# Attention stage: weighted sums in two halves, maxima turned on VectorE, output normalised on GpSimd by feature, jumps announced

## What is computed

```
h = layernorm(x) * (1 + ca) + sa
Q, K, V = lora_linear(h, ...)          # (4, 2048, 16 heads, 16)
scores = Q K^T / sqrt(16) + 0.5**head * (pos_k - pos_q)
attn = softmax(scores, axis=-1)        # over 2048 keys
out = lora_linear(attn V, Wo, bo, Ao, Bo)
x = x + ga * (h + rezero * out)
```

## Time and profile before

| | us |
|---|---|
| median of 3 runs (5603.05 to 5615.82) | 5609.89 |
| the profiled execution, its own time | 5616.02 |
| its span | 5614.2 |
| TensorE (PE) busy, of the span | 5090.5 (91%) |
| VectorE (DVE) busy | 4278.1 (76%) |
| ScalarE (ACT) busy | 3127.8 (56%) |
| GpSimd (POOL) busy | 1232.7 (22%) |

### The profile page before, as it was taken

The page is one execution under the profiler, slowest core; times in us unless marked ns, Lnnn a source line. Parts: engine busy times, 40 slices in busy tenths (PEclk is TensorE's granted clock), DMA queues, the critical chain, the costliest instruction groups (busy, mean ns, idle before and its releaser), DMA issues. The chain is left out here.

```text
span 5614.2 us, 90199 instructions
## 1 busy us (share of the span) xinstructions
PE 5090.5 (91%) x27025; PEld 2743.7 (49%) x27025; DVE 4278.1 (76%) x6749; ACT 3127.8 (56%) x5877; POOL 1232.7 (22%) x959
## 2 busy tenths in 40 slices
PE   5859999999999999999999878987799999956998
PEld 3723333333333333333333367776565555645666
DVE  4768888888888888888888768787798898974000
ACT  1317777777777777777778623232444445433111
POOL 1310000000000000000000033333565666643222
PEclk8959999999999999999999989998889899956999
DMA  4850222202222022220222121112000000034443
GB/s 138 288 122 6 35 57 35 49 13 35 57 35 48 14 35 57 34 47 15 35 57 34 33 55 34 45 34 67 24 18 19 26 18 19 25 130 146 149 147 101
DMA packets 226907, 328.00 MB, mean 58 GB/s; under 512 B 58516, under 2 KB 176527, under 8 KB 216697
## 3 DMA queue, kind: packets, MB, share of 16 engines
q1 hardware_dynamic: 214300, 264.56, 19.8%
q0 software_dynamic: 12224, 58.43, 2.8%
HBM read 195.90 MB, written 134.59 MB: 59 GB/s over the span
## 5 line engine op out<-in xcount | busy, mean ns | idle before, releaser
L667 DVE TENSOR_REDUCE at_mxp<-at_ps_m 128x2 f32<-128x1024 f32 x2098 | 2462.4, 1218 | 379.8 <-PE at_ps_m L726 373.9
L617 ACT ACTIVATE at_prob<-at_ps_s 128x512 f32<-128x512 f32 x4100 | 2114.3, 603 | 482.8 <-PE at_ps_s L716 481.9
L716 PE MATMUL at_ps_s<-at_qs,at_ks 51*128 51x512 f32 x4100 | 1443.1, 477 | 27.7 <-issue 17.0
L716 PEld LDWEIGHTS at_ps_s<-at_qs,at_ks 51*128 51x128 f32 x4100 | 576.6, 186 | 1273.4 <-ACT at_prob L617 1109.7
L734 PE MATMUL at_ps_o<-at_prob,at_vs 128*32 128x512 f32 x8192 | 1104.3, 611 | 0.0
L726 PE MATMUL at_ps_m<-at_ks,at_qs 49*128 49x512 f32 x4196 | 958.4, 429 | 73.3 <-DMA at_vs<-t_v 51.5
L551 POOL TENSOR_TENSOR at_onorm<-at_otok,at_rec 128x256 f32<-128x256 f32 x65 | 40.2, 618 | 2271.3 <-DVE at_rec L682 2271.3
L726 PEld LDWEIGHTS at_ps_m<-at_ks,at_qs 49*128 49x128 f32 x4196 | 431.7, 190 | 161.5 <-DVE at_mxp L667 73.5
L1200 PE MATMUL mi_ps_f<-mi_w,mi_act 128*128 128x256 f32 x1024 | 262.5, 402 | 58.5 <-DVE mi_acc L1033 58.5
L2314 ACT ACTIVATE ex_hid<-ex_ps_h,ex_b 128x512 f32<-128x512 f32 x128 | 87.9, 687 | 386.9 <-PE ex_ps_h L2330 386.9
L734 PEld LDWEIGHTS at_ps_o<-at_prob,at_vs 128*32 128x32 f32 x8192 | 161.8, 108 | 258.5 <-ACT at_prob L617 191.4
(11 more groups left out here) (310 smaller groups left out, 6284.5 us busy)
## 6 DMA issues: line engine op xcount, KB each, us to landing
t_parts<-pr_parts SPq DMA_DIRECT2D x64, 512.0 KB, 4.8
ex_w<-in_fw SPq DMA_DIRECT2D x32, 1024.0 KB, 7.4
at_qs<-t_parts SPq DMA_DIRECT2D x102, 256.0 KB
at_ks<-t_parts SPq DMA_DIRECT2D x102, 256.0 KB
t_buf<-at_blank POOLq DMA_DIRECT2D x8, 3076.0 KB, 9.2
at_vs<-t_v SPq DMA_DIRECT2D x17, 1024.0 KB
ex_rest<-t_buf SPq DMA_DIRECT2D x16, 1026.0 KB, 5.1
t_v<-pr_vaug SPq DMA_DIRECT2D x64, 256.0 KB, 4.9
```

Source lines behind the costliest of these rows:

```text
L617: nc.scalar.activation(prob[0 if n is None else (t + 1) % 2][:, j, :], bank[:, :], ACT.Exp).then_inc(s_read, 1)
L667: nc.vector.tensor_reduce(out[:, s4, k + i, 2 * pair:2 * pair + 2], ps_m[i][:, :, :], AX.X, ALU.max).then_inc(mx_read, 1)
L716: nc.tensor.matmul(bank[:, :], ks[s][a:a + QROWS, j // 2, t1 * P:(t1 + 1) * P], qs[s][a:a + QROWS, j // 2, c * T:(c + 1) * T], start=True, ...
```

## The change

1. **Step order.** A step was scores 0, 1, maxima pair 0, score 2, maxima pair 1, score 3, weighted sums over 512 queries. It becomes scores 0, 1, maxima pair 0, weighted sums over queries 0 to 255, scores 2, 3, maxima pair 1, weighted sums over queries 256 to 511.
2. **Maxima.** `max_rows` and `take_rows` go. VectorE turns blocks of 32x32 (`turn`, at step 8, after `neg_cut`), SyncE writes them to DRAM and reads them back as rows.
3. **Normalisation.** `sums_by_token`, `take_tokens` and `invert` go. SyncE shifts the 16 sum rows of each head beside its feature rows by four transfers into `weight` (`shift_sums`); GpSimd raises `weight` (128x512) to the power -1 and multiplies it with `osum` (128x512). The output is stored by feature, four transfers per chunk, and mix loads it as it is: its `attention_rows` go. The bias of V is added in the projection instead.
4. **Waits.** `take_sums(n)` waits for `norm_done`; `turn` waits for `neg_cut`.
5. **Loads and blank rows in portions:** a quarter of the next unit's loads in every chunk, and a 128x769 piece of the blank rows instead of 128x6152 in every eighth.
6. **Loops.** Every loop is made with a hint for its jump back; the attend loops hold 16 chunks (TensorE, ScalarE, GpSimd and SyncE had 8, VectorE 2).

```diff
+def loop(nc, eng, first, end):
+    return nc.Fori(first, end, engines=[eng.engine], hint_back_edge=True)
...
-                    nc.vector.tensor_copy(vaug[h][:, 2 * half:2 * half + 2, :, 0:HD],
-                                          ps_v[half][:, :, :].rearrange("p s (h e) -> p s h e", e=HD)).then_inc(v_out, 1)
+                    for s in range(2):
+                        last = nc.vector.tensor_tensor(vaug[h][:, 2 * half + s, :, 0:HD], ps_v[half][:, s, :].rearrange("p (h e) -> p h e", e=HD),
+                                                       bv[:, :].rearrange("p (h e) -> p h e", e=HD), ALU.add)
...
                 def normalise(n, r, m):
-                    pool.wait_ge(rec_done, n + 1)
-                    pool.wait_ge(o_stored[r], 16 * m)
-                    nc.gpsimd.tensor_tensor(onorm[r][:, :, :].rearrange("p s (j c) -> p s j c", j=HPG), otok[:, :, :, 0:HD],
-                                            rec[:, :, :].unsqueeze(3).to_broadcast([P, SUB, HPG, HD]), ALU.mult).then_inc(norm_done, 1)
+                    pool.wait_ge(sums_in, 16 * HPG * (n + 1))
+                    nc.gpsimd.tensor_tensor(weight[:, :], weight[:, :], minus[:, :].to_broadcast([P, T]), ALU.pow)
+                    pool.drain()
+                    pool.wait_ge(o_stored[r], 16 * HPG * m)
+                    nc.gpsimd.tensor_tensor(onorm[r][:, :], osum[:, :], weight[:, :], ALU.mult).then_inc(norm_done, 1)
...
+                with loop(nc, pool, 0, TURNS) as up:
+                    for r in range(CH):
+                        n = up * CH + r
+                        nc.gpsimd.dma_start(d["buf"][ds(n * P, P), :], blank[:, :]).then_inc(cleared, 16)
+                        normalise(n, r % 2, up * (CH // 2) + r // 2)
                         cut_largest(n + 1)
...
+                        for c in range(QC):
                             n = u * QC + c
+                            shift_sums(n)
+                            if c < len(CUTS):
+                                load_band((u + 1) % UNITS, 1 - s, c)
+                            else:
+                                load_values((u + 1) % UNITS, 1 - s)
+                            store_rows(n, c % 2)
+                            store_max(n + 1, (c + 1) % 2, s if c < QC - 1 else 1 - s, (c + 1) % QC)
...
                 def take_sums(n):
+                    act.wait_ge(norm_done, n)
                     act.wait_ge(o_done, n)
                     nc.scalar.copy(osum[:, :], ps_o[:, :]).then_inc(o_out, 1)
...
+                def turn(n):
+                    dve.wait_ge(turned_out, 16 * n)
+                    dve.wait_ge(neg_cut, n + 1)
+                    nc.vector.transpose(nturned[:, :], nparts[:, :, :, :].rearrange("p j e s -> p (j e s)").bitcast(F32)).then_inc(turned, 1)
...
                             if t == NEXT:
-                                negate(n + 1, 1 - r)
-                            maxima(n, r, t + LEAD)
-                invert(UNITS * QC, UNITS * QC * JOBS + len(FIRST))
+                                negate((r + 1) % 2)
+                            if t == NEXT + 1:
+                                turn(n + 1)
+                            maxima(n, r % 2, t + LEAD)
```

More of the change, by code:

```diff
@@ L420, in _ @@
                 modulate(0, 0)
-                with act.Fori(0, B) as b:
+                with loop(nc, act, 0, B) as b:
                     for c in range(CPB):
@@ L512, in attend_phase, with bank_of, place @@
         NEXT = 2 * TILES - LEAD
-        T_SUMS, T_INV, T_ROWS = 2, 4, NEXT + 4
         assert TILES == KT
[L515 to L528, removed]
+        NLD = 4 * len(CUTS) + HPG
+        LU = 4
+        TURNS = UNITS // LU
+        CH = LU * QC
+        JOBS = HPG * KT
+        LOOP = CH * JOBS
+        def bank_of(k):
+            return (k + (LOOP % RING == 1 and k >= LOOP // 2)) % RING
+        def place(up, n, t, j):
+            k = (n * KT + t) * HPG + j
+            if up is None:
+                return j, bank_of(LOOP - HPG + j), 0
+            back = next(a for a in range(1, LOOP) if bank_of((k - a) % LOOP) == bank_of(k))
+            return HPG + up * LOOP + k, bank_of(k), back
         def tile(t):
@@ L599, in _ @@
+                with loop(nc, sp, 0, TURNS) as up:
+                    for uu in range(LU):
+                        s = uu % 2
+                        u = up * LU + uu
                         for c in range(QC):
                             n = u * QC + c
-                            wait_alone(sp, norm_done, n + 1, always)
-                            sp.dma_start(d["o"][ds(n, 1), :, :, :].rearrange("n p s c -> p (n s) c"), onorm[c % 2][:, :, :]).then_inc(o_stored[c % 2], 16)
-                            sp.wait_ge(s_read, place(n, "rows", T_ROWS)[0] + 1)
@@ L632, in take_tokens @@
-                def take_tokens(n, last):
-                    i, bank = place(n, "sums", T_SUMS)
-                    act.wait_ge(s_done, i + 1 if not last else UNITS * QC * JOBS + len(FIRST) + 1)
-                    act.wait_ge(norm_done, n)
-                    nc.scalar.copy(otok[:, :, :, :].rearrange("p s j c -> p (s j c)"), (bank if not last else ps_s[LASTB])[:, :]).then_inc(s_read, 1)
-                LASTB = len(FIRST) % RING
                 act.wait_ge(always, 1)
-                take_rows(None, True)
@@ L724, in max_scores @@
                     q0 = c * T + s4 * P
-                    for a in order:
+                    for a in range(2):
                         last = nc.tensor.matmul(ps_m[i][:, a, :], qs[s][a * 64:a * 64 + MXR, pair, q0:q0 + P],
@@ L878, in _ @@
                 load_x(2, 0)
-                with sp.Fori(0, B) as b:
+                with loop(nc, sp, 0, B) as b:
                     for c in range(CPB):
@@ L1055, in _ @@
                 first_norm(1, 1, 2)
-                with dve.Fori(0, B) as b:
+                with loop(nc, dve, 0, B) as b:
                     dve.drain()
@@ L1210, in _ @@
                 up(0, 0, 1)
-                with pe.Fori(0, B) as b:
+                with loop(nc, pe, 0, B) as b:
                     for c in range(CPB):
@@ L2144, in _ @@
                 columns(0)
-                with act.Fori(0, B - 1) as b:
+                with loop(nc, act, 0, B - 1) as b:
                     batch(b, False)
@@ L2308, in _ @@
             def _(act):
-                with act.Fori(0, PAIRS) as m:
+                with loop(nc, act, 0, PAIRS) as m:
                     for h in range(2):
```

325 lines of the change are left out of this document (143 added, 182 removed).

## The result

The changed kernel takes **10187.3 us** (median of 4 runs, 10160.92 to 10212.81), the kernel before on the same chip 5612.9 (4 runs): a ratio of **1.8141** (95% interval 1.8094 to 1.8188). The forecast was 9888 within 9000 to 10,900. The profiled execution took 10160.92 us, its span is 10159.3.

A forecast was written before the change was run, and what follows sets the result against it. TensorE bounds attention now, VectorE close behind; after the change the chunk waits for GpSimd's power. From 5616.0: 64 x (109.8 - 43.9) = 4218, + 85, - 25 = 9894, less 6 for the median: 9888 us, range 9000 to 10,900.

The forecast's parts named there:

- The price of the power: GpSimd's power over 512 columns in the normalisation: 81.4 us, from a slope of 0.158 us per column.
- rival 1: The power on GpSimd is as cheap as a multiplication: 5361 us, faster than before; chance 0.12.
- The chain: Attention, one chunk from one o_done to the next, its waits in sequence: 109.8 us against 43.9 before; chance 0.73.
- copy and shift: Start of an attention chunk: copy of sums 0.6 us, then SyncE's four transfers 3.2 us.
- from the turn to the next copy: End of an attention chunk: turn 0.2, first late reduction 1.2, TensorE's remaining steps 17.2, lower clock 4 us.
- Rival 3: TensorE stays at 1.2 GHz after each standstill in attention: 13 us more per chunk, 10,720 us; chance 0.05.
- The end: Last normalisation of attention, exposed: 90 us where 5.3 stood, so + 85.
- The rest: Outside attention: 15 us gained from mix's dropped transposes, plus three later-stage jumps at 3.4 us; - 25 in all.
- Rival 4: turn does not hold VectorE in attention, if the cut ran first: 86.8 us per chunk, 8420 us; chance 0.02.
- the bare cycle: An attention chunk of only copy, shift, power, multiplication and signal: 0.6 + 3.2 + 81.4 + 1.5 + the signal = 86.8 us.
- Step and hint: Attention steps take 2.5 us instead of 2.61; fewer loop edges and the hint nearly pay for the jumps.
- Two of the signs: In attention's profile: GpSimd busy for over 90%, TensorE's clock at 0.5 in over half of the slices.

The follow-up runs named there:

- e1: The changed kernel with GpSimd's power replaced by a multiplication of the same width, so the output lacks its reciprocals: 5425.5 us, ratio 0.9663.
- e4_compact: The changed kernel with the sums laid out as 128x16, raised to the power there, written to DRAM and read back: 5576.3 us, ratio 0.9927.
- f1: e4_compact with the portion of the next unit's loads issued right behind the first transfer of the sums: 5438.3 us, ratio 0.9687.
- f2: f1 with eight unread transposes per chunk on TensorE in the mix stage, where attention_rows stood: 5389.5 us, ratio 0.9600.
- f4: f1 without the hint for the jumps back in every loop, the loops as long: 5462.3 us, ratio 0.9724.

## Why the prediction was right, and where its numbers were off

**The price of the power** was the step that decided, and it held: 81.93 us for 81.4. The second point of the study (41.13 us for 256 columns) makes it a line through four widths: 1.01, 2.91, 41.13 and 81.93 us for 4, 16, 256 and 512. The rule of the Trainium skill weighed there (GPSIMD Engine Reference, Performance versus the Vector engine) was measured on an addition, and fits e1's multiplication, 1.03 us for 512 columns, roughly. The power takes 80 times that (81.93/1.03), so one rate for all operations does not hold here. Its consequence, rival 1, falls with it.

**The chain** held link by link, and as a sum: 112.93 us per chunk ((7625.8 - 398.2)/64) against 109.8. Of the 3.1 us, means over all chunks:
- copy and shift 4.97 for 3.8: + 1.2. The copy of the chunk above starts at 2988.68, its power at 2993.24 (4.6), and in other chunks SyncE came up to 2 us later;
- from the power's start to the turn 83.67 for 83.4: + 0.3;
- from the turn to the next copy 24.29 for 22.6: + 1.7. The size that was wrong is that of the clock. After TensorE resumed, the lower level held for 3.7 to 25.4 us over the 64 chunks, 13.0 on the mean, and it cost 5.7 us (24.29 less the 18.6 of the terms without the clock) where I had 4.

I took the 6.8 us of the earlier trace rows, which is the first of the seven jumps before the change. At the other six the lower level held for 10.2 us, so the sample was the shortest one in the trace. The second jump:

```profile
1099.10:1109.30 10.20, 9.75 (x38) 4.69 (x40) 4.71 (x4) 4.93 (x10) 0.00 (x0) 0.50 1.03 125
```

The length of the standstill does not explain the rest: in e4_compact the lower level stood for up to 23.9 us around waits of 2.1 to 3.6 us.

Two such ends of a chunk in the changed kernel, with the same 168 matmuls:

```profile
4997.20:5026.70 29.50, 28.18 (x168) 9.34 (x170) 18.91 (x17) 13.95 (x26) 0.46 (x1) 0.55 0.06 20
6135.00:6155.20 20.20, 18.84 (x168) 6.93 (x170) 18.99 (x17) 13.99 (x26) 0.50 (x1) 0.87 0.10 29
```

At a granted clock of 0.55 they take 29.5 us, at 0.87 20.2. Rival 3 (the clock does not come back) is thus real in 9 of the 64 chunks, where the granted clock is 0.55 to 0.57, and false on the mean. Its price was too high: these ends take at most 29.6 us from turn to copy, 7 above the forecast's 22.6 and not 13, since a half step at the lower level takes 2.16 us for 1.24 and not twice as long.

**The end** held: from the last copy of sums (7625.8) until the last output store is issued 90.3 us, for 90.

**The rest: − 15 for mix had the wrong sign.** The stage went from 699.7 to 742.3 us in the changed kernel; in the eight other kernels without transposes there it takes 738.4 to 753.5. I counted the transposes as time on the path. They also kept TensorE at work where it now waits for ScalarE's copy of the mask (`mi_maskT`). The groups by line of the mix stage, in f1 and then in f2; the last number before the releaser is the idle time ahead of the group:

```profile
L1177 PE MATMUL mi_ps_f<-mi_w,mi_act 128*128 128x256 f32 x1024 | 283.5, 426 | 60.3 <-DVE mi_acc L1027 60.3
L1166 PE MATMUL mi_ps_h<-mi_hTc,mi_w1c 128*128 128x512 f32 x780 | 241.7, 449 | 7.7 <-POOL mi_hTc L67 7.7
...
L1197 PE MATMUL mi_ps_a<-mi_b,mi_maskT 8*128 8x256 f32 x128 | 48.0, 535 | 10.7 <-ACT mi_maskT L1111 10.7
```

```profile
L1177 PE MATMUL mi_ps_f<-mi_w,mi_act 128*128 128x256 f32 x1024 | 262.6, 402 | 60.1 <-DVE mi_acc L1027 60.1
L1166 PE MATMUL mi_ps_h<-mi_hTc,mi_w1c 128*128 128x512 f32 x780 | 224.7, 424 | 7.7 <-POOL mi_hTc L67 7.7
...
L1202 PE MATMUL mi_ps_a<-mi_b,mi_maskT 8*128 8x256 f32 x128 | 31.8, 387 | 0.0
```

The wait for the mask is only 10.7 us in sum. The matmuls behind it are the loss: the same counts of the same shapes take 54 us more (21 + 17 + 16) in f1, at the lower granted clock. The kernel before has the means of f2 (402 ns for the first shape), the changed kernel 419; over the whole stage the granted clock is 0.93 before and 0.86 after, with 136 matmuls fewer (2812, 2676). f2 shows that it is the missing work and not the new layout of the output: it keeps the layout, adds work without use, and is back at 702.2.

The forecast was low by 299 us: 201 for the chunks (they grew by 4419.5 us, not 4218), 58 for mix (42.6 + 15), 8 for the other stages and the end, and 32 because the median lies 26 us above the profiled run where I had it 6 below. The scan came 10.2 us shorter (1017.6 to 1007.4), as I had counted for its jumps (10). That was in part luck: TensorE's waits behind its three jumps are 6.3 us shorter in sum than before, and f1 against f4 shows 3.3 us of the stage from the hint; what made the rest was not looked for.

The Trainium skill says (TensorE: Matmul & The Clock Gate, Part 1) that the clock follows how busy TensorE has lately been. The two windows above agree: f1 has 2429 matmuls in 640 us at a granted clock of 0.87, f2_fill_mix 2742 at 0.96.

**Rival 1**, had the power been cheap, would have been 5425 and not 5361: its chunk was right (40.04 for 40.4), its mix was not. **Rival 4** was wrong in its mechanism: with the cut off GpSimd the kernel takes 9323, not 8420. I had named what stands behind the power in GpSimd's queue and missed, for this rival, what stands behind the stores in SyncE's, though the order has `store_max` behind `store_rows` and the chain itself counted the stores ahead of the maxima. With both removed the bare cycle appears (8726, 90.45 us per chunk for 86.8).

**Step and hint** held: 2.48 us, no long gap on TensorE in attention, and VectorE's gaps at the jumps of the scan gone.

**Two of the signs** named for the profile did not come, although the chain did. GpSimd is busy for 74% of attention (5371.6 of 7227.6 us) and not for over 90%; the chain itself gave 76% (83.0/109.8). And no slice shows a clock of 0.5: a slice of 254 us covers more than two chunks, and the slices stand at 0.6 to 0.7, with 0.66 over the whole of attention. The others came: 65 powers, TensorE's stop behind step 9, and VectorE idle before the turn, for 67.6 us against "some 60".

Left open: why the full clock comes back after 4 us in one chunk and after 25 in another. No kernel was made for it.

## What to carry to other kernels

When an operation is made wider, take its price per column from two widths of the same operation in the trace; a rate for "elementwise" work would have missed this one by a factor of some 80. Then walk through every in-order queue that the long operation touches and ask what stands behind it, and behind whatever waits for it: here a subtraction on one queue and a row placement on another each tied the whole kernel to it, and removing one showed only the other. And work that TensorE does inside a wait may be holding its clock: removing it lost 50 us, and putting useless work there gave them back.

## What was not expected of the hardware

- The power on GpSimd costs 0.159 us per column over 128 partitions from 4 columns to 512, with a spread of 33 ns over 65 instructions; a multiplication of the same shape in the same place takes 1.03 us.
- Eight unread transposes per chunk made the mix stage 50 us shorter (752.6 to 702.2), at a granted clock of 0.96 for 0.87.
- After standstills of the same kind (66.6 to 68.9 us in all chunks but the first) TensorE's lower level lasted from 3.7 to 25.4 us. Two chunks, one with 0.50 three times in a row, the other with 0.64 over the first 7 us and then 1.00:

```profile
4997.20:5004.20 7.00, 5.68 (x34) 1.89 (x34) 5.27 (x6) 2.04 (x4) 0.46 (x1) 0.50 0.26 80
5004.20:5011.20 7.00, 7.00 (x45) 2.25 (x38) 4.19 (x4) 3.38 (x7) 0.00 (x0) 0.50 0.01 2
5011.20:5018.20 7.00, 7.00 (x40) 2.45 (x40) 3.86 (x4) 3.25 (x6) 0.00 (x0) 0.50 0.00 0
```

```profile
6135.00:6142.00 7.00, 5.64 (x38) 1.94 (x38) 5.80 (x6) 2.20 (x5) 0.50 (x1) 0.64 0.26 80
6142.00:6149.00 7.00, 7.00 (x72) 2.64 (x72) 6.99 (x7) 6.29 (x12) 0.00 (x0) 1.00 0.01 4
```
